# Attention with decay masks: row maxima split on GpSimd, turned onto the stack's partitions, far keys first, max pass 10 slots ahead

## The chip, the cores and the metric

The kernel runs on one core of one Trainium2 chip. The metric is the device time of one execution in microseconds (us), median over runs. Engines are named as in the profile: PE is TensorE (PEld its weight loads), DVE is VectorE, ACT is ScalarE, POOL is GpSimd, SP is SyncE, which issues most DMAs. A letter q behind an engine's name (ACTq, SPq) marks a DMA that this engine issues.

## What is computed

One transformer layer over x of shape (2, 2048, 256): a layer norm, attention with 16 heads of 16 values, an output projection and a residual, then a layer norm, a two-matrix FFN with ternary weights and a residual. The attention weights its scores with a decay that depends on the distance of query and key, one mask per head:

```python
attn_scores = jnp.einsum('bhqd,bhkd->bhqk', q, k) / jnp.sqrt(jnp.float32(D))
time_diffs = jnp.abs(t[:, None] - t[None, :])
decay_masks = dp[:, :, None, None] ** time_diffs[None, None, :, :]
decay_mask = jnp.einsum('hnqk,hn->hqk', decay_masks, mix)
attn_scores = attn_scores * decay_mask[None]
attn_probs = jax.nn.softmax(attn_scores, axis=-1)
out = jnp.einsum('bhqk,bhkd->bhqd', attn_probs, v)
```

The masked scores are wanted twice: once for their maximum over the keys of each query, once, with that maximum subtracted, for the exponential.

## The kernel before, in words

A first block (`token_block`, to about 110 us) makes the layer norm, the projections and the decay tables and builds the first pair of heads. A second block holds attention and the FFN. Attention takes 16 **steps** (2 batches x 8 pairs of heads; `for_steps`, line 810). A step has 4 **units** (2 heads x 2 halves of 1024 queries) of 8 **slots**; in a slot two blocks of 128 keys are worked on, against the 1024 queries of the unit.

Two passes run through the same slots (the tensor block's `step`, lines 1785 to 1817):

- The **scores** (`scores`, line 1649): scores lie transposed, keys on partitions. A key block and a query half that don't share the same half of the sequence ("far") are one matmul of 512 columns per tile, with the decay built into the operands at level 0. A near block is made of levels 1, 2 and 3 (512, 256 and 128 columns) and of its 128 x 128 diagonal square, which is brought in by a transpose (line 1661). The operands are the **stacks** `q_stack` and `k_stack`: 96 rows of high and low f16 parts, and two more rows (96 and 97, `STACK` to `STACK + MAXROWS`) that multiply a constant of the k side with the high and low part of minus the query's maximum over 1024, so that the maximum is subtracted by the matmul itself. A slot has four tiles of 128 x 512 in a ring of three PSUM banks (`tile`); ScalarE takes each through an exponential (line 1379) into `probs`, and a slot later TensorE multiplies `probs` with the values (`values`, line 1687).
- The **max pass** runs `LEAD` = 12 slots ahead (`max_scores`, line 1621): queries on partitions, 128 of them against 2048 keys a slot, in two items of 1024 keys. VectorE multiplies each item with the head's mask and reduces it to a maximum (`max_block`, line 1408; line 1425). The item that holds the diagonal is written to `masked` (two buffers), from which GpSimd copies the diagonal square (`keep_diag`, line 1201; line 1207). TensorE may not run ahead of VectorE by more than the `ring` of two items.

Slots count from 0 to 31 in a step. Eight blocks of the max pass belong to one unit. After the eighth, in slot 4 of every 8 (`RED_SLOT`), VectorE reduces the items to `row_max` (`finish_max`, line 1429; line 1434) and splits it into two f16 parts for all four levels (`split_max`, line 1436; lines 1443 and 1447). In the next slot (`TURN_SLOT`) TensorE transposes the 64 columns of `max_parts` (`turn_max`, line 1641; line 1646) into a tile bank, as one more item of the tile ring between the slot's third and fourth tile; ScalarE copies 64 x 128 values into `max_rows` (`take_turn_max`, line 1346; line 1351) and issues a DMA that lays them out in the two rows of `q_stack` for all four levels (`store_max_rows`, line 1354; line 1357). GpSimd subtracts the maxima from the unit's eight diagonal squares (`diag_minus_max`, line 1209; line 1213). The unit that uses all this starts in the next slot with s % 8 == 0; there TensorE waits for the stacks' loads, that row DMA (`rows_in`) and the diagonals (`diag_ready`), lines 1790 to 1797. Key blocks are taken in their order, 0 to 15, in both halves.

Meanwhile the next pair's operands are built in eight chunks: GpSimd multiplies (line 289), ScalarE casts to f16 (line 302), GpSimd subtracts for the low part (line 308). `pool_slot` and `cast_slot` (lines 1002 to 1007) write out by hand in which slot of a step each of these is issued; each engine works in the order of its program. SyncE's order is written out too (`step`, lines 1099 to 1166): stack 1 at a step's start, the next masks and raw heads when the max pass is done with the old, levels 0 and 1 and then 2 and 3 of stack 0, and last the tables and q and k of the pair after (`builder.load`, line 197). In the last step nothing of this is built and the first pieces of the FFN are mixed into the slots.

Of the kernel before, what the change touches and what calls it, by code (L numbers as in the profile page):

```python
# [792 lines left out]
LEAD = UNIT_SLOTS + 4  # L793
# [4 lines left out]
RED_SLOT, TURN_SLOT = 4, 5  # L798
# [41 lines left out]

def score_parts(block, side):
# [12 lines left out]
def attention_and_ffn_block(nc, a, keep, builder, proj, scr, out):  # L854
# [7 lines left out]
    with ExitStack() as ctx:  # L862
# [17 lines left out]
        max_parts = sb("max_parts", [P, MAXROWS, DEPTH, UNIT_SLOTS], F16)  # L880
        max_rows = sb("max_rows", [MAXROWS * DEPTH * UNIT_SLOTS, P], F16)
        unit = sb("unit", [P, 1])
        zero = sb("zero", [P, 1])
# [56 lines left out]
        max_ready, max_hi, parts_ready = sem("max_ready"), sem("max_hi"), sem("parts_ready")  # L940
# [12 lines left out]
        const_in, zero_ready = sem("const_in"), sem("zero_ready")  # L953
# [4 lines left out]
        LO_ROWS = DEPTH * UNIT_SLOTS  # L958
# [36 lines left out]
        def place(g):  # L995
# [6 lines left out]
        pool_slot = {2: ("product", 0), 4: ("product", 1), 7: ("rest", 0), 8: ("product", 2), 10: ("rest", 1),  # L1002
                     11: ("product", 3), 12: ("rest", 2), 14: ("product", 4), 15: ("rest", 3), 16: ("product", 5),
                     18: ("rest", 4), 19: ("product", 6), 20: ("rest", 5), 22: ("product", 7), 24: ("rest", 6),
                     26: ("rest", 7)}
        cast_slot = {5: (0, 0), 6: (0, 1), 7: (1, 0), 8: (1, 1), 9: (2, 0), 10: (2, 1), 12: (3, 0), 13: (3, 1),
                     15: (4, 0), 16: (4, 1), 17: (5, 0), 18: (5, 1), 20: (6, 0), 21: (6, 1), 23: (7, 0), 24: (7, 1)}

        @block.sync
        def _(sp):  # L1010
# [88 lines left out]
            def step(i, o, more):  # L1099
# [59 lines left out]
                if i + 2 < STEPS:  # L1159
                    builder.load(sp, i + 2)  # L1160
# [33 lines left out]
        def _(pool):  # L1194
# [14 lines left out]
            def diag_minus_max(h, half, count):  # L1209
# [4 lines left out]
                                        ALU.subtract).then_inc(diag_ready, 1)  # L1214

# [53 lines left out]
            for s in range(-LEAD, 0):  # L1269
                keep_diag(s, 0)  # L1270
                if s == TURN_SLOT - UNIT_SLOTS:
                    diag_minus_max(0, 0, 1)
            def step(i, o, more):
                for s in range(SLOTS):
# [3 lines left out]
                    if s % UNIT_SLOTS == TURN_SLOT and (more or u < UNITS):  # L1278
                        diag_minus_max((u // 2) % 2, u % 2, UNITS * i + u + 1)
# [29 lines left out]
        def _(act):  # L1309
# [36 lines left out]
            def take_turn_max(slot, o, count):  # L1346
# [7 lines left out]
            def store_max_rows(h, half, slot, o):  # L1354
# [6 lines left out]
            take_turn_max(TURN_SLOT - UNIT_SLOTS, 0, 1)  # L1361
            store_max_rows(0, 0, TURN_SLOT - UNIT_SLOTS, 0)
            proj.wait_rows(act, GROUPS)
            def step(i, o, more):
# [5 lines left out]
                for s in range(SLOTS):  # L1370
# [3 lines left out]
                    for x in range(4):  # L1374
                        n = tile_item(s, x, o)
                        if turning and x == 3:
                            take_turn_max(s, o, UNITS * i + u + 1)
# [4 lines left out]
                    if turning:  # L1382
                        store_max_rows(u // 2 % 2, u % 2, s, o)
# [23 lines left out]
        def _(dve):  # L1407
# [27 lines left out]

            def split_max(par, count):

                hi, lo = max_parts[:, 0], max_parts[:, 1]
                row = row_max[:, par].unsqueeze(1).broadcast_to([P, DEPTH, UNIT_SLOTS])
                dve.wait_ge(max_ready, count)  # L1440
                if count > 1:
                    dve.wait_ge(rows_in, QUADS * (count - 1))
                nc.vector.scalar_tensor_tensor(out=hi, in0=row, scalar=-1.0 / MAXUNIT,  # L1443
# [445 lines left out]
```

## Time and profile before

| | us |
|---|---|
| runs, median (lowest to highest, 3 runs) | 1913.11 (1912.32 to 1914.3) |
| the profiled execution, its own time | 1910.07 |
| its span, first to last instruction | 1908.3 |
| granted clock of TensorE, mean | 0.95 of full speed |

Durations below are from that one execution. A line such as L1425 is a line of the kernel. "out<-in" names tensors without their buffer numbers; `late` is the shared memory that holds the second stacks and `probs`. In a timeline row the bracket at the end is the idle time just before and what ended it; PE rows with a count merge several matmuls that overlap. PEclk is the granted share of TensorE's clock in a stretch: 1.0 is 2.4 GHz, 0.5 is 1.2 GHz, and a value between is a stretch with both.

### The profile page before, as it was taken

Reading aid. Unit: us, or ns where it says so; the run is one execution under the profiler, and the core shown is the slowest. Engines: PE = TensorE matmul, PEld = TensorE weight load, DVE = VectorE, ACT = ScalarE, POOL = GpSimd, SP = SyncE. Lnnn points to the kernel's source line nnn. Section 1 sums busy time; section 2 is a strip of 40 time slices with the busy share of each in tenths; the row PEclk is TensorE's granted clock in tenths of the full one; section 3 lists DMA queues with packets and bytes.
Section 4 is the critical chain, followed back from the end, with each engine's and each line's share of the span. In section 5 each row is a group of like instructions: output and inputs, shape, how many; then the busy total and the mean of one; then the engine's idle time right before and its main releaser. Section 6 shows DMA issues by size and latency. Waiting matters only on the chain.

```text
span 1908.3 us, 31293 instructions
## 1 busy us (share of the span) xinstructions
PE 1705.1 (89%) x10834; PEld 589.1 (31%) x10834; DVE 1527.7 (80%) x2638; ACT 1427.4 (75%) x2669; POOL 912.7 (48%) x915
## 2 busy tenths in 40 slices
PE   7836899998989899989898989899999999999998
PEld 5401222222222222223232222222222222224666
DVE  5766888787878787878787888888887878796885
ACT  6524878787878787878787878778787878787665
POOL 6733637363636454555545464636373636343010
PEclk9867999999999999999999999999999999999999
DMA  6967574756565665748484757575747575562640
GB/s 206 331 205 187 149 169 126 179 136 170 144 159 146 151 160 146 178 120 198 116 192 131 177 141 173 148 168 144 174 130 183 129 178 143 139 186 59 159 125 34
DMA packets 195217, 300.03 MB, mean 157 GB/s; under 512 B 92114, under 2 KB 115538, under 8 KB 184914
## 3 DMA queue, kind: packets, MB, share of 16 engines
q1 hardware_dynamic: 188980, 296.85, 61.1%
q10 hardware_dynamic: 6080, 1.19, 0.4%
q8 instruction: 86, 1.41, 0.3%
q14 instruction: 71, 0.58, 0.1%
HBM read 152.18 MB, written 42.99 MB: 102 GB/s over the span
## 4 chain that ended last, share of the span: by engine, by line
PE 59%; DVE 15%; issue 9%; DMA 5%; SPq 3%; ACT 2%; POOL 1%; DVEq 0%; ACTq 0%
PE tile L1664 21%; PE ring L1679 20%; PE ring L1633 11%; DVE masked L1425 5%; DMA late<-max_rows 4%; DVE unseen L1425 4%; DVE max_parts L1443 3%; PE tile L1661 2%; PE ring L1749 2%; SPq L233 1%; ACT late L1379 1%; PE tile L1731 1%; SPq L202 1%; DVE qk L1514 1%; DMA raw_scratch<-late 1%
## 5 line engine op out<-in xcount | busy, mean ns | idle before, releaser
L1379 ACT ACTIVATE late<-tile 128x512 f32<-128x512 f32 x2048 | 1107.6, 604 | 321.1 <-PE tile L1664 219.5
L1425 DVE CUSTOM_DVE_ANT_0 masked<-ring,mask 128x1024 f32<-128x1024 f32 x512 | 625.0, 1221 | 180.7 <-PE ring L1633 158.1
L1425 DVE CUSTOM_DVE_ANT_0 unseen<-ring,mask 128x1024 bf16<-128x1024 f32 x512 | 625.0, 1221 | 100.1 <-PE ring L1633 100.1
L1679 PE MATMUL ring<-late,v_ones 128*32 128x512 f32 x4096 | 569.7, 629 | 0.1
L1207 POOL COPY diag<-masked 128x128 f32<-128x128 f32 x512 | 149.0, 291 | 780.3 <-DVE part_max L1425 769.6
L1633 PE MATMUL ring<-k_raw,q_raw 64*128 64x512 f16 x2048 | 351.6, 397 | 88.9 <-DVE part_max L1425 76.7
L1664 PE MATMUL tile<-late 98*128 98x512 f16 (+2 forms) x1280 | 330.0, 345 | 62.2 <-issue 48.0
L1664 PE MATMUL tile<-q_stack,k_stack 98*128 98x512 f16 (+2 forms) x1280 | 316.8, 334 | 11.6 <-ACT late L1379 8.5
L289 POOL TENSOR_TENSOR decayed<-qk,table_in 128x1024 f32<-128x1024 f32 x120 | 284.1, 2367 | 2.4 <-DMA table_in<-table_scratch 2.3
L308 POOL TENSOR_TENSOR lo<-decayed,hi 128x1024 f16<-128x1024 f32 x120 | 256.3, 2136 | 0.0
L1664 PEld LDWEIGHTS tile<-late 98*128 98x128 f16 x1280 | 101.7, 99 | 389.7 <-ACT late L1379 239.7
L1664 PEld LDWEIGHTS tile<-q_stack,k_stack 98*128 98x128 f16 x1280 | 100.0, 98 | 316.0 <-ACT late L1379 214.0
L302 ACT CAST hi<-decayed 128x512 f16<-128x512 f32 (+1 forms) x248 | 158.3, 638 | 21.8 <-DMA late<-lo 10.5
L1633 PEld LDWEIGHTS ring<-k_raw,q_raw 64*128 64x128 f16 x2048 | 91.9, 94 | 267.4 <-DVE part_max L1425 151.0
L1661 PE MATMUL tile<-ident,diag 128*128 128x128 f32 x512 | 143.8, 281 | 0.0
L1679 PEld LDWEIGHTS ring<-late,v_ones 128*32 128x32 f32 x4096 | 82.0, 109 | 170.7 <-issue 130.7
L1213 POOL TENSOR_TENSOR diag<-diag,row_max 128x1024 f32<-128x1024 f32 x64 | 121.4, 1897 | 0.1
L1425 DVE DVE_READ_ACCUMULATOR2_ANT part_max<- 128x1 f32 x1024 | 84.1, 82 | 0.0
L1661 PEld LDWEIGHTS tile<-ident,diag 128*128 128x128 f32 x512 | 72.4, 141 | 6.6
L1218 POOL TENSOR_TENSOR diag<-diag,bo_all 128x1024 f32<-128x1024 f32 x8 | 18.8, 2354 | 110.0 <-DMA diag<-in_x 110.0
L1514 DVE TENSOR_TENSOR qk<-late,diag 128x512 f16<-128x512 f32 x64 | 45.3, 709 | 27.9 <-ACT late L1337 27.9
L1443 DVE SCALAR_TENSOR_TENSOR max_parts<-row_max,zero 128x32 f16<-128x32 f32 x64 | 56.1, 877 | 2.4 <-DVE row_max L1434 0.3
(148 smaller groups left out, 1049.1 us busy)
## 6 DMA issues: line engine op xcount, KB each, us to landing
mask<-mask_row_scratch SPq DMA_DIRECT2D x128, 496.0 KB, 7.5
table_in<-table_scratch SPq DMA_DIRECT2D x64, 256.0 KB, 8.4
q_raw<-raw_scratch SPq DMA_DIRECT2D x128, 128.0 KB
k_stack<-hi SPq DMA_DIRECT2D x64, 256.0 KB, 4.0
q_stack<-hi SPq DMA_DIRECT2D x128, 128.0 KB, 3.8
late<-hi SPq DMA_DIRECT2D x64, 256.0 KB, 8.7
late<-hi SPq DMA_DIRECT2D x128, 128.0 KB, 8.0
out_scratch<-heads_out SPq DMA_DIRECT2D x64, 256.0 KB, 6.2
```

The lines of the kernel that those rows point to most:

```text
L289: ops.tensor_tensor(self.source(c), self.half_view(self.qk[:], level, side), self.factors(level, side), ALU.mult).then_inc(self.decayed_re ...
L302: self.nc.scalar.copy(out, src).then_inc(self.hi_ready, 2 if x is None else 1)
L308: ops.tensor_tensor(self.half_view(self.lo[:, level], level, side), self.source(c), self.half_view(self.hi[:, level], level, side), ALU.su ...
L1207: nc.gpsimd.tensor_copy(diag[h][:, q], masked[:, b % 2, at:at + P]).then_inc(masked_free, 1)
L1213: nc.gpsimd.tensor_tensor(part, part, row_max[:, half].unsqueeze(2).broadcast_to([P, UNIT_SLOTS, P]), ALU.subtract).then_inc(diag_ready, 1)
L1379: nc.scalar.activation(probs[:, (2 * s + x // 2) % 4, x % 2 * 512:(x % 2 + 1) * 512], tile[:, n % TILE_BANKS], ACT.Exp, scale=1.0 / (SCALE ...
L1425: nc.vector.tensor_tensor_reduce(out=masked[:, b % 2] if diagonal else unseen[:], in0=pair, in1=factor, scale=1.0, scalar=-3.0e38, op0=ALU ...
L1443: nc.vector.scalar_tensor_tensor(out=hi, in0=row, scalar=-1.0 / MAXUNIT, in1=zero[:].unsqueeze(2).broadcast_to([P, DEPTH, UNIT_SLOTS]), op ...
L1633: last = nc.tensor.matmul(ring[:, 2 * (n % RING) + r], q_raw[h][rows, q * P:(q + 1) * P], k_raw[h][rows, k], start=True, stop=True)
L1661: last = nc.tensor.matmul(out, diag[h][:, kb], ident[:], is_transpose=True, start=(j == 0), stop=True, skip_group_check=True)
L1664: last = nc.tensor.matmul(out, k_stack[h][:, level, kb * P:(kb + 1) * P], q_stack[h][:, half, level, first - half * HALF:first - half * HA ...
L1679: last = nc.tensor.matmul(acc[row:row + ROWS], v_ones[h][:, t % BLOCKS], probs[:, t % 4, qt * 512:(qt + 1) * 512], start=(j % UNIT_SLOTS = ...
```

## The change

The maxima are split by GpSimd instead of VectorE, three small operations into an f16 tile that holds only the two parts of 8 x 128 maxima. TensorE turns them with eight transposes, block by block, whose output lies on PSUM partitions 96 and 97, the partitions of the stack's two rows, 1024 f16 values wide. ScalarE copies that straight into level 0 of `q_stack`, and the DMA that follows only copies level 0 to levels 1 to 3. Keys are taken far half first (`key_block`), so that a unit's first four slots need level 0 alone; the waits for levels 2 and 3 of the stacks, for that DMA and for the diagonals go to the unit's fifth slot (`NEAR_SLOT`). The max pass leads by 10 slots, which puts reduction, turning and the diagonals' subtraction into slots 5, 6 and 7 of every 8. The slots of products, rests and casts are written anew, and SyncE issues the loads of the pair after next before the last output store and the second half of stack 0. `last_turn` gives the tile item of a turn, for the waits on ScalarE's copy.

```diff
-LEAD = UNIT_SLOTS + 4
+LEAD = UNIT_SLOTS + 2
...
-RED_SLOT, TURN_SLOT = 4, 5
+RED_SLOT = (UNIT_SLOTS - 1 - LEAD) % UNIT_SLOTS
+TURN_SLOT = RED_SLOT + 1
+NEAR_SLOT = UNIT_SLOTS // 2
+DIAG_SLOT = UNIT_SLOTS - 1
...
+def key_block(t, half):
+
+    return (t + (1 - half) * UNIT_SLOTS) % BLOCKS
...
+        pool_slot = {3: ("product", 0), 6: ("product", 1), 8: ("rest", 0), 9: ("product", 2), 11: ("rest", 1),
+                     12: ("product", 3), 14: ("rest", 2), 16: ("product", 4), 17: ("rest", 3), 18: ("product", 5),
+                     19: ("rest", 4), 20: ("product", 6), 22: ("rest", 5), 24: ("product", 7), 25: ("rest", 6),
+                     27: ("rest", 7)}
+        cast_slot = {5: (0, 0), 7: (0, 1), 9: (1, 0), 10: (1, 1), 11: (2, 0), 12: (2, 1), 13: (3, 0), 15: (3, 1),
+                     17: (4, 0), 18: (4, 1), 19: (5, 0), 20: (5, 1), 21: (6, 0), 23: (6, 1), 25: (7, 0), 26: (7, 1)}
...
                     load_max_pass(1, i + 1)
+                if i + 2 < STEPS:
+                    sp.wait_ge(builder.decayed_ready, CHUNKS * (i + 2))
+                    builder.load(sp, i + 2)
                 store_out(i, 2)
...
                     load_q(0, 1, 1)
-                if i + 2 < STEPS:
-                    builder.load(sp, i + 2)
...
+            def split_max(par, slot, o, count):
+
+                hi, lo = max_parts[:, :, 0], max_parts[:, :, 1]
+                pool.wait_ge(max_ready, count)
+                if count == 1:
+                    pool.wait_ge(unit_ready, 1)
+                if count > 1:
+                    pool.wait_ge(exp_done, last_turn(slot + 1, o) + TILE_BANKS + 1)
+                nc.gpsimd.tensor_tensor(max_neg[:], row_max[:, par], down_unit[:].broadcast_to([P, UNIT_SLOTS]), ALU.mult
+                                        ).then_inc(neg_ready, 1)
+                pool.wait_ge(neg_ready, count)
+                nc.gpsimd.tensor_copy(hi, max_neg[:]).then_inc(max_hi, 1)
+                pool.wait_ge(max_hi, count)
+                nc.gpsimd.tensor_tensor(lo, max_neg[:], hi, ALU.subtract).then_inc(parts_ready, 1)
...
-                    if s % UNIT_SLOTS == TURN_SLOT and (more or u < UNITS):
+                    if s % UNIT_SLOTS == RED_SLOT and (more or u < UNITS):
+                        split_max(u % 2, s, o, UNITS * i + u + 1)
+                    if s % UNIT_SLOTS == DIAG_SLOT and (more or u < UNITS):
                         diag_minus_max((u // 2) % 2, u % 2, UNITS * i + u + 1)
...
-                act.wait_ge(rows_in, QUADS * (count - 1))
-                nc.scalar.copy(max_rows[:], tile[0:MAXROWS * LO_ROWS, n % TILE_BANKS, 0:P // 2].bitcast(F16)
-                               ).then_inc(exp_done, 1)
...
+                nc.scalar.copy(q_stack[h][STACK:STACK + MAXROWS, half, 0],
+                               tile[STACK:STACK + MAXROWS, n % TILE_BANKS].bitcast(F16)).then_inc(exp_done, 1)
...
-                act.dma_start(q_stack[h][STACK:STACK + MAXROWS, half], max_rows[:]).then_inc(rows_in, QUADS)
+                act.dma_start(q_stack[h][STACK:STACK + MAXROWS, half, 1:DEPTH],
+                              q_stack[h][STACK:STACK + MAXROWS, half, 0].unsqueeze(1).broadcast_to([MAXROWS, DEPTH - 1, HALF])
+                              ).then_inc(rows_in, QUADS)
...
-                        split_max(u % 2, UNITS * i + u + 1)
...
-                nc.tensor.transpose(tile[0:MAXROWS * LO_ROWS, n % TILE_BANKS, 0:P // 2].bitcast(F16),
-                                    max_parts[:].rearrange("p r l b -> p (r l b)"), keep["ident16"][:]).then_inc(tile_full, 1)
+                for b in range(UNIT_SLOTS):
+                    last = nc.tensor.transpose(tile[STACK:STACK + MAXROWS, n % TILE_BANKS, b * P // 2:(b + 1) * P // 2].bitcast(F16),
+                                               max_parts[:, b], keep["ident16"][:])
+                last.then_inc(tile_full, 1)
...
-                u, kb = t // BLOCKS, t % BLOCKS
+                u = t // BLOCKS
                 h, half = u // 2, u % 2
+                kb = key_block(t % BLOCKS, half)
...
-                        for done in (*(k_in[u // 2] if u % 2 == 0 else ()), *q_in[u // 2][u % 2]):
+                        pe.wait_ge(exp_done, last_turn(TURN_SLOT + s, o) + TILE_BANKS + 1)
+                        for done in (k_in[u // 2][0], q_in[u // 2][u % 2][0]):
                             pe.wait_ge(done, PART_DMAS * QUADS * (i + 1))
...
+                    if s % UNIT_SLOTS == NEAR_SLOT:
+                        u = s // UNIT_SLOTS
+                        for done in (k_in[u // 2][1], q_in[u // 2][u % 2][1]):
+                            pe.wait_ge(done, PART_DMAS * QUADS * (i + 1))
                         pe.wait_ge(rows_in, QUADS * (UNITS * i + u + 1))
                         pe.wait_ge(diag_ready, UNITS * i + u + 2)
```

## Rows read from the trace of the kernel before

**Rows 1.** The page's first part: engine, busy us (share of the span), instructions.

```profile
PE 1705.1 (89%) x10834; PEld 589.1 (31%) x10834; DVE 1527.7 (80%) x2638; ACT 1427.4 (75%) x2669; POOL 912.7 (48%) x915
```

**Rows 2.** The page's fourth part: the chain of waits, by engine and by line.

```profile
PE 59%; DVE 15%; issue 9%; DMA 5%; SPq 3%; ACT 2%; POOL 1%; DVEq 0%; ACTq 0%
...
PE tile L1664 21%; PE ring L1679 20%; PE ring L1633 11%; DVE masked L1425 5%; DMA late<-max_rows 4%; DVE unseen L1425 4%; DVE max_parts L1443 3%; PE tile L1661 2%; PE ring L1749 2%; SPq L233 1%; ACT late L1379 1%; PE tile L1731 1%; SPq L202 1%; DVE qk L1514 1%; DMA raw_scratch<-late 1%
```

**Rows 3.** Windows, line 1379 (exponentials) alone, steps 1 to 14: start:end, us, busy (count).

```profile
265.72:1660.72 1395.00, 969.70 (x1792) 0.96 0.63 155
```

**Rows 4.** Windows, step 8: start:end, length, busy (count) PE, PEld, DVE, ACT, POOL; PEclk, DMA share, GB/s.

```profile
967.02:980.71 13.69, 13.68 (x96) 4.50 (x94) 12.06 (x22) 11.26 (x22) 5.45 (x7) 1.00 1.04 224
...
980.71:984.81 4.10, 3.02 (x19) 0.76 (x17) 4.07 (x7) 3.01 (x6) 2.60 (x3) 1.00 1.00 222
...
990.18:1003.75 13.57, 13.57 (x88) 3.88 (x87) 12.23 (x23) 12.73 (x27) 9.39 (x10) 1.00 0.61 179
...
1003.75:1008.32 4.57, 3.12 (x22) 1.09 (x21) 4.57 (x6) 3.02 (x8) 2.17 (x3) 1.00 0.24 93
...
1011.06:1015.02 3.96, 2.87 (x24) 1.04 (x22) 3.57 (x7) 2.68 (x6) 3.47 (x3) 1.00 0.08 25
...
1015.02:1028.70 13.68, 13.67 (x96) 4.45 (x94) 10.90 (x20) 12.90 (x25) 9.25 (x10) 1.00 0.71 149
...
1028.70:1033.42 4.72, 3.07 (x19) 0.76 (x17) 4.68 (x7) 3.05 (x7) 3.22 (x3) 1.00 0.15 53
...
1033.42:1037.57 4.15, 4.15 (x18) 0.65 (x16) 2.02 (x5) 2.18 (x5) 2.81 (x3) 0.59 0.92 257
...
1037.57:1042.85 5.28, 2.70 (x18) 0.67 (x16) 4.15 (x8) 2.68 (x6) 2.15 (x3) 1.00 0.69 197
...
1042.85:1046.62 3.77, 3.77 (x17) 0.67 (x16) 0.91 (x1) 3.14 (x7) 0.52 (x1) 0.62 0.13 52
...
1057.81:1060.68 2.87, 2.87 (x22) 1.10 (x21) 2.62 (x5) 2.43 (x5) 0.80 (x2) 1.00 0.86 223
```

**Rows 5.** The tile max_parts: ns minimum/median/maximum, first and last start, form.

```profile
L1443 DVE SCALAR_TENSOR_TENSOR max_parts<-row_max,zero x64: 191/192/2004, 141.7 to 1715.4; 128x32 f16<-128x32 f32 x64
...
L1447 DVE SCALAR_TENSOR_TENSOR max_parts<-row_max,max_parts x64: 191/192/2040, 141.9 to 1715.6; 128x32 f16<-128x32 f32 x64
```

**Rows 6.** Timeline, step 8, slot 12 to 13: start, us, engine, line, operation.

```profile
1002.98 2.14 POOL L308 TENSOR_TENSOR lo<-decayed,hi 128x1024 f16<-128x1024 f32 x1
...
1003.13 2.04 DVE L1447 SCALAR_TENSOR_TENSOR max_parts<-row_max,max_parts 128x32 f16<-128x32 f32 x1
```

**Rows 7.** Timeline, step 8, slots 21 to 24, the row DMA and TensorE's next score.

```profile
1030.98 0.56 ACTq L1357 DMA_DIRECT2D late<-max_rows  x1
...
1042.37 0.81 PE L1664 MATMUL tile<-late 98*128 98x512 f16 x3 [2.58 <-issue]
```

**Rows 8.** Timeline, step 8, slots 28 and 29: reduction and transpose.

```profile
1056.91 0.17 DVE L1434 TENSOR_REDUCE row_max<-part_max 128x8 f32<-128x16 f32 x1
...
1059.13 0.11 PEld L1646 LDWEIGHTS tile<-ident,max_parts 128*64 128x64 f16 x1 [0.84 <-ACT late L1379]
```

**Rows 9.** Groups by line and form: busy us, mean ns | idle before, releaser.

```profile
L289 POOL TENSOR_TENSOR decayed<-qk,table_in 128x1024 f32<-128x1024 f32 x120 | 284.1, 2367 | 2.4 <-DMA table_in<-table_scratch 2.3
...
L1326 ACT CAST mask<-ring 128x1024 f16<-128x1024 f32 x8 | 8.1, 1011 | 3.4 <-PE ring L1715 3.4
...
L1351 ACT COPY max_rows<-tile 64x128 f16<-64x128 f16 x64 | 16.5, 258 | 32.5 <-PE tile L1646 31.9
...
L480 POOL TENSOR_TENSOR power<-power 32x8 f32<-32x8 f32 x1 | 0.2, 195 | 0.1
```

**Rows 10.** Timeline, last step: four matmuls of 128 columns.

```profile
1742.43 0.39 PE L1773 MATMUL ring<-ident,hi 128*128 128x128 f16 x4
```

**Rows 11.** Timeline, step 0: the first score, and the cast of slot 5.

```profile
152.75 0.48 PE L1664 MATMUL tile<-q_stack,k_stack 98*128 98x256 f16 x2 [3.08 <-DMA q_stack<-max_rows]
...
180.93 0.62 ACT L302 CAST hi<-decayed 128x512 f16<-128x512 f32 x1 [10.54 <-DMA late<-lo]
```

More of the change, by code:

```diff
@@ L838, in items_done, with last_turn @@
     return RING_STEP * o + ring_item(slot, ITEMS - 1) + AHEAD_ITEMS + 1
+def key_block(t, half):
+    return (t + (1 - half) * UNIT_SLOTS) % BLOCKS
+def last_turn(slot, o):
+    if slot < 0 or (slot == TURN_SLOT and o == 0):
+        return 0
+    return turn_item(slot - UNIT_SLOTS, o) if slot >= UNIT_SLOTS else turn_item(slot + SLOTS - UNIT_SLOTS, o - 1)
 def score_parts(block, side):
@@ L879, in attention_and_ffn_block @@
         row_max = sb("row_max", [P, 2, UNIT_SLOTS])
-        max_parts = sb("max_parts", [P, MAXROWS, DEPTH, UNIT_SLOTS], F16)
-        max_rows = sb("max_rows", [MAXROWS * DEPTH * UNIT_SLOTS, P], F16)
+        max_neg = sb("max_neg", [P, UNIT_SLOTS])
+        max_parts = sb("max_parts", [P, UNIT_SLOTS, MAXROWS], F16)
         unit = sb("unit", [P, 1])
-        zero = sb("zero", [P, 1])
+        down_unit = sb("down_unit", [P, 1])
         warm = sb("warm", [P, 1])
@@ L1270, in _ @@
                 keep_diag(s, 0)
-                if s == TURN_SLOT - UNIT_SLOTS:
+                if s == RED_SLOT - UNIT_SLOTS:
+                    split_max(0, s, 0, 1)
+                if s == DIAG_SLOT - UNIT_SLOTS:
                     diag_minus_max(0, 0, 1)
@@ L1434, in finish_max @@
                 nc.vector.tensor_reduce(row_max[:, par], part_max[:, par], AX.X, ALU.max).then_inc(max_ready, 1)
[L1436 to L1443, printed above, removed]
-                                               in1=zero[:].unsqueeze(2).broadcast_to([P, DEPTH, UNIT_SLOTS]),
-                                               op0=ALU.mult, op1=ALU.add).then_inc(max_hi, 1)
-                dve.wait_ge(max_hi, count)
-                nc.vector.scalar_tensor_tensor(out=lo, in0=row, scalar=-1.0 / MAXUNIT, in1=hi, op0=ALU.mult,
-                                               op1=ALU.subtract).then_inc(parts_ready, 1)
             def invert(g):
@@ L1559, in _ @@
                 max_block(s, 0)
-                if s % UNIT_SLOTS == RED_SLOT and s + LEAD >= UNIT_SLOTS:
+                if s == RED_SLOT - UNIT_SLOTS:
                     finish_max(0, items_done(s, 0), None)
-                    split_max(0, 1)
             def step(i, o, more):
@@ L1678, in products @@
                         row = (2 * par + qt) * ROWS
-                        last = nc.tensor.matmul(acc[row:row + ROWS], v_ones[h][:, t % BLOCKS],
+                        last = nc.tensor.matmul(acc[row:row + ROWS], v_ones[h][:, key_block(t % BLOCKS, u % 2)],
                                                 probs[:, t % 4, qt * 512:(qt + 1) * 512],
@@ L1780, in _ @@
                 max_scores(s, range(ITEMS), 0)
-                if s % UNIT_SLOTS == TURN_SLOT and s + LEAD >= UNIT_SLOTS:
+                if s == TURN_SLOT - UNIT_SLOTS:
                     turn_max(s, 0, 1)
```

28 lines of the change are left out of this document (11 added, 17 removed).

## The prediction

> **What bounds the kernel now.** I read the engine shares first: TensorE is busy 89% of the span [rows 1]. The chain of waits is on TensorE for 59%, but also 15% on VectorE, 9% in "issue" and 5% on DMA, where it names the DMA that carries the row maxima into the stack (4%) and the line on VectorE that splits them (3%) [rows 2]. So I went to the attention stage, 14 whole steps of which take 1395.00 us: 1792 exponentials, four to a slot, 448 slots, 99.64 us a step [rows 3].
>
> Then one step in stretches, cut at the first exponential of a slot [rows 4]. Three stretches of five slots have TensorE busy without a gap (13.68 of 13.69 us) at full clock: 40.94 us for 15 slots, **2.73 us a slot, 87.4 a step**. VectorE has 10.9 to 12.2 and ScalarE 11.3 to 12.9 busy us in the same stretches, so TensorE is the limit there. Of the missing 12.3 us, 11.6 sit in eight slots. Over 2.73 each:
> - slots 5, 13, 21 (4.10, 4.57, 4.72): +1.37, +1.84, +1.99. These are the slots in which a unit's maxima are reduced, split and turned; TensorE is busy only 3.0 to 3.1 us in them.
> - slot 15 (3.96): +1.23, and slot 23 (5.28): +2.55, each the last before a unit starts.
> - slots 22 and 24 (4.15, 3.77): +1.42 and +1.04 with TensorE busy throughout, at a granted clock of 0.59 and 0.62: part of each at the lower level (1.2 GHz), right after the stalls of 21 and 23.
> - slot 29 (2.87), also a turning slot: +0.14 only.
>
> Why does slot 29 cost a tenth of the other three? The two split operations on VectorE take 0.19 us at the least and median, but up to 2.00 and 2.04 [rows 5]. In slot 13 the second one runs from 1003.13 for 2.04 us and ends at 1005.17, 0.05 us after a GpSimd subtraction that began at 1002.98 and took 2.14 [rows 6]. VectorE is held by GpSimd's operation, and the max pass, and TensorE behind it, with it. In slot 29 GpSimd has no product or rest to do. The slots ahead of a unit's start wait for the row DMA: issued at 1030.98, TensorE goes on at 1042.37 after an idle 2.58, 11.4 us later; slots 22 and 23 hide only part of it [rows 7].
>
> **The change, part by part.**
> - *Split moved to GpSimd.* Removed from VectorE: two operations a unit, 0.38 us free, up to 2.2 held. The VectorE operations that stay are not held: in two clean stretches 22 and 23 of them take 12.06 and 12.23 us, beside 5.45 and 9.39 us of GpSimd [rows 4]. Added on GpSimd: three operations of 8 columns, 0.195 us each by the nearest row (32x8) [rows 9], 0.6 us, and some 0.3 for the waits between them. In the clean turning slot the reduction starts at 1056.91 (0.17 long) and TensorE loads the transpose at 1059.13 [rows 8]: 2.22 us, so 2.22 - 0.17 - 0.9 = 1.15 are to spare and TensorE does not wait. Behind GpSimd's new wait stand the next diagonal copy (VectorE needs it only two blocks later) and the products; GpSimd has no product or rest in slots 5, 13, 21 and 29 by the new table.
> - *Turning.* One transpose becomes eight of 128 columns. Four such matmuls in a row take 0.39 us [rows 10], one alone 0.219 [rows 9], so they start 0.055 apart: seven more, +0.39 on TensorE. ScalarE's copy grows from 128 columns (0.258) to 1024 on two partitions; a 1024-column copy from PSUM takes 1.011 [rows 9]: +0.75. Nothing (ScalarE is busy 11.26 of 13.69 us in five slots without casts [rows 4], so 0.49 idle a slot, and the new cast table has none in turning slots) and all of it are the bounds. There are three tile banks: after the transposes TensorE has one score tile (0.22 by the spacing above), the next slot's four max matmuls (0.44 to 0.88, as their two row halves run side by side or not) and another tile before it needs the bank that this copy holds, 0.9 to 1.3 us against a copy that ends some 1.2 after; the copy then puts off the exponential behind it and so the next bank. That is nearer the middle than either end; I take +0.40. A turning slot is then 2.87 + 0.39 + 0.40 = 3.66, **0.93 over a plain slot** (bounds 3.26 and 4.01).
> - *Maxima into level 0 by ScalarE, spread to levels 1 to 3 by DMA; far keys first.* A unit's first four slots read level 0 alone. Its start waits for a copy made a slot and a half earlier: nothing. The DMA is now awaited in the unit's fifth slot, some five slots (13.6 us) after its issue instead of two; where it is slowest it takes the 11.4. So +1.23 and +2.55 go. What is late next: the diagonal (GpSimd subtracts in slot 7, TensorE wants it in slot 12) and levels 2 and 3 of the stacks, wanted four slots later than now.
> - *Clock.* With the stalls of 21 and 23 gone, +1.42 and +1.04 go too. After the stalls of 5 and 13, of 1.4 and 1.8 us, the rows that follow show 1.00 [rows 4], so stalls of about half a microsecond should not lower it.
> - *SyncE.* Six loads of the next pair go ahead of the output store and nine stack loads, behind a wait for the last product (slot 24). The stack loads wait for the rests (slot 27) anyway, and the store is needed two units later: nothing. The moved casts and products are the same in number: nothing.
> - *Lead 10 for 12.* Two slots fewer of max pass at the start; but step 0 stands in slot 5 until 180.93 for a load into the second stack [rows 11], which depends on no score. I count nothing; the bound is a gain of 8: two slots at VectorE's 12.06 / 5 = 2.41 [rows 4] and the 3.08 that the first score waits for the row DMA [rows 11]. At the end two more slots carry four 512-column max matmuls, at most 2 x 4 x 0.22 = 1.8; I take 1.
>
> **The sum.** A step: 87.4 + 4 x 0.93 = 91.1, against 99.64: 8.5 saved, x14 = 120. Step 0 after its load: 26 slots took 265.7 - 181.5 = 84.2; 26 x 2.73 + 3 x 0.93 = 73.8: 10.4 saved. The last step has no products to hold VectorE: three turning slots 0.79 dearer each, and the 1 us: 3.4 lost. Together 127. The profiled execution took 1910.07 (span 1908.3), so 1783; the median of the runs is 3.04 higher: **1786**. With the cheap turning slot: 89.5 a step, 1762, and with all of the start 1754. With the dear one: 92.5 a step, 1808.
>
> **Rivals.**
> - *The clock still falls.* If the new stalls of turning slots keep a drop of the kind of slots 22 and 24, 2.46 us a step come back: x14 = 34, **1820**. For it: TensorE still waits there. Against: slots 5 and 13.
> - *The spread lands late.* It decides from about 14 us on. From slot 29 on and in the next step's first slots the DMA engines are 0.86 to 1.04 busy [rows 4]. At 20 us one unit a step waits 6: +84, **1870**. Against: its 11.4 us came under a like load. The Trainium skill (DMA: Bandwidth & Descriptors, Rules for kernel authors) says that a small outermost dimension confines a DMA to as many engines; by it the two rows ride on two engines behind everything queued there, as today's would not less, so the 11.4 agrees but bounds nothing.
> - *VectorE stays held.* If it is not the split alone that GpSimd's work holds up, the 1.37 to 1.99 stay: 4.8 us a step, +67, **1853**. Against: the two clean stretches of the part on the split.
> - *Slower: the split comes late.* GpSimd runs in order. If it is two large operations behind when the maxima come (2.4 + 2.1 us), the split ends 4.5 - 1.15 = 3.4 us after TensorE wants it, in three units, and each such stall costs 1.4 us more of low clock: 3 x 4.8 = 14.4 us a step, x14 = 202, **1988**. One operation behind costs about 1.2 and still gains; the sign turns where each of three units loses 3 us (127 / 14 / 3). For it: products and rests stand in slots 16 to 20 without a break, 2.37 us for a product [rows 9] and a diagonal copy beside it. Against: 2.73 a slot holds that. The Trainium skill (GPSIMD Engine Reference, Performance versus the Vector engine) keeps elementwise work on VectorE, GpSimd being about 1.96 times slower: an estimate by it makes the split 2 x 1.96 x 0.19 = 0.75 us; the rows here give 0.6 for three operations, and both fit the 1.15 to spare, so it is the queue and not the operation that this case hangs on.
>
> **How the numbers follow.** The forecast gets 0.74, the clock 0.08, a late spread 0.05, VectorE held 0.06, slower 0.05, no difference 0.02. A measurement of this kernel can tell 0.2% (3.8 us). The first four are faster: 0.93. The range goes from 1756 (the cheap turning slot and most of the start) past the dear one and the clock's case to 1838; beyond it lie the late spread, the held VectorE, the slower and the null case, 0.18.
>
> **What would show it.** Right: slots 5, 13, 21 gone from the stalls and slots 6, 14, 22, 30 all alike at 3.3 to 4.0; no wait of TensorE on the row DMA; clock 1.00 through slots 21 to 25; about 91 us a step; VectorE's line for the split gone and no other of its lines slower. Wrong: TensorE waiting for GpSimd's split or, in a unit's fifth slot, for a DMA; ScalarE's wide copy over 1.1 us; a step above 96.

## The result, and the profile after

The changed kernel takes **1934.06 us** (median of 4 runs, 1927.67 to 1937.88); the kernel before, run beside it, 1913.7 (4 runs, 1912.32 to 1920.8). The ratio is **1.0095, interval 1.0055 to 1.0136**: slower by about 1%. Forecast were 1786, range 1756 to 1838, and 0.05 for slower. The profiled execution took 1927.67 us (span 1925.9), 17.6 more than that of before.

First the page's engine shares and its chain by engine, which answer to [rows 1, 2]:

```profile
PE 1697.7 (88%) x11282; PEld 614.7 (32%) x11282; DVE 1448.3 (75%) x2510; ACT 1468.2 (76%) x2669; POOL 952.1 (49%) x1107
...
PE 41%; SPq 20%; DMA 19%; DVE 5%; ACT 4%; issue 3%; POOL 2%; ACTq 0%; DVEq 0%; POOLq 0%
```

VectorE has gone from 15% of the chain to 5%, as it should; but DMA and SyncE's queue have come from 8% to 39%. The same 14 steps as in [rows 3], then step 8 cut by slots (columns as in [rows 4]; 0 to 2, 3, 4, 5, 6, 7 to 13, 14, 15 to 21, 22, 23 to 29, 30, 31):

```profile
255.37:1672.94 1417.57, 972.98 (x1792) 0.95 0.64 153
...
966.44:974.38 7.94, 7.94 (x50) 1.97 (x48) 7.20 (x13) 6.91 (x13) 1.81 (x4) 1.00 1.03 211
974.38:985.90 11.52, 2.98 (x19) 0.99 (x18) 4.14 (x8) 2.17 (x4) 2.87 (x3) 0.79 0.79 189
985.90:990.88 4.98, 4.98 (x21) 1.36 (x20) 1.10 (x1) 2.17 (x4) 0.00 (x0) 0.50 0.55 134
990.88:993.90 3.02, 3.02 (x22) 1.03 (x20) 1.96 (x6) 2.56 (x5) 0.86 (x4) 0.95 0.88 154
993.90:997.50 3.60, 3.43 (x31) 1.47 (x28) 2.82 (x5) 3.20 (x6) 2.61 (x2) 1.00 0.33 91
997.50:1016.43 18.93, 18.93 (x125) 5.62 (x124) 16.40 (x30) 18.16 (x35) 13.23 (x15) 1.00 0.51 150
1016.43:1020.00 3.57, 3.40 (x31) 1.45 (x28) 2.87 (x5) 3.20 (x6) 1.79 (x3) 1.00 0.13 52
1020.00:1038.75 18.75, 18.75 (x125) 5.64 (x125) 16.29 (x30) 18.01 (x35) 16.29 (x17) 1.00 0.42 97
1038.75:1042.36 3.61, 3.44 (x31) 1.48 (x28) 2.83 (x5) 3.20 (x6) 2.44 (x3) 1.00 0.56 90
1042.36:1061.21 18.85, 18.85 (x124) 5.60 (x124) 16.32 (x30) 16.97 (x32) 10.84 (x14) 1.00 0.80 189
1061.21:1064.86 3.65, 3.48 (x32) 1.48 (x30) 2.95 (x5) 3.18 (x5) 0.48 (x2) 1.00 1.02 214
1064.86:1067.50 2.64, 2.64 (x19) 0.76 (x19) 1.89 (x5) 2.17 (x4) 1.24 (x2) 1.00 1.01 261
```

A step is 101.26 us (1417.57 / 14), not 91.1. Everywhere but in slots 3 to 5 the forecast stands: plain slots 2.64 to 2.70 by the mean of each row, turning slots 3.57 to 3.65 and all alike, no wait at a unit's start, clock 1.00. All of the loss lies in unit 0: slot 3 takes 11.52 and slot 4, at clock 0.50, 4.98 (12.21 and 4.58 by the mean of the 14 steps). (A slot is cut at ScalarE's first exponential, so a wait of TensorE in its slot 4 shows in slot 3.) The view of waits, and TensorE's timeline in step 9, say for what:

```profile
PE tile L1687 <- DMA q_stack<-lo: 128.9, 14, 12.1
...
POOL decayed L289 <- DMA table_in<-table_scratch: 71.1, 15, 7.5
...
1086.31 0.48 PE L1687 MATMUL tile<-q_stack,k_stack 98*128 98x256 f16 x2 [8.66 <-DMA q_stack<-lo]
```

In 14 steps TensorE waits 9.2 us on average for levels 2 and 3 of stack 0. Against before: the start and step 0 gain 10.2 us (first exponential of step 1 at 255.4 instead of 265.6), 14 steps lose 22.5 (1417.57 - 1395.09, cut alike), and the last step with what follows it loses the other 5.3.

**Why so late?** SyncE issues these loads at 1057.0 to 1066.8, slots 28 to 31; the last that unit 0 needs goes out at 1060.74, 17 us before TensorE wants it (at 1077.65, the end of its wait less 8.66). The issues of that stretch in the DMA view (count, KB each, median us to landing):

```profile
k_stack<-hi SPq DMA_DIRECT2D x2, 256.0 KB, 19.5
q_stack<-hi SPq DMA_DIRECT2D x4, 128.0 KB, 11.7
out_scratch<-heads_out SPq DMA_DIRECT2D x1, 256.0 KB, 26.2
k_stack<-lo SPq DMA_DIRECT2D x1, 256.0 KB, 13.0
q_stack<-lo SPq DMA_DIRECT2D x2, 128.0 KB, 23.8
```

Loads of one size, issued within 10 us, take 12 us or 24 (the six of 128 KB). The trace counts the arrivals on a semaphore in order of time, so a share that lags shows only at the last load of each semaphore; q_stack<-lo is the third of three. Some of the 16 engines are about 12 us behind the rest. Which, is in the step's own row of slot 14: SyncE has issued nothing for 9 us, and the DMA share is still 0.13, 52 GB/s. 0.13 x 16 = **two engines**, 26 GB/s each. Slots 6 to 8 issued one head's raw q and k: 4 loads of 128 KB and 4 of 64, 786 kB, 15.1 us at 52 GB/s. In the changed kernel the other head's raw loads are issued from 1038.0, its masks from 1044.9, and then, without a pause, the six loads and the nine. The two engines carry their sixteenth of all these behind 15 us of raw loads.

### The profile page after: what moved, and what is told of

It reads as the page before. It is cut to its first block, busy times and chain, and to the rows that moved or that the text cites. A ratio compares the mean times of both kernels' runs of the same rounds, so it can differ in the third digit from the quotient of the medians.

```text
span 1925.9 us, 32286 instructions
## 1 busy us (share of the span) xinstructions
PE 1697.7 (88%) x11282; PEld 614.7 (32%) x11282; DVE 1448.3 (75%) x2510; ACT 1468.2 (76%) x2669; POOL 952.1 (49%) x1107
## 4 chain that ended last, share of the span: by engine, by line
PE 41%; SPq 20%; DMA 19%; DVE 5%; ACT 4%; issue 3%; POOL 2%; ACTq 0%; DVEq 0%; POOLq 0%
DMA q_stack<-lo 18%; PE ring L1702 14%; PE tile L1687 14%; PE ring L1653 7%; SPq L233 5%; SPq L86 4%; SPq L213 3%; SPq L77 3%; SPq L202 2%; SPq L75 2%; PE ring L1772 2%; POOL decayed L289 2%; DVE masked L1462 2%; PE tile L1684 1%; PE tile L1754 1%
## 5 line engine op out<-in xcount | busy, mean ns | idle before, releaser
L1702 PE MATMUL ring<-late,v_ones 128*32 128x512 f32 x4096 | 559.6, 618 | 5.2 <-issue 5.1
L1687 PE MATMUL tile<-q_stack,k_stack 98*128 98x512 f16 (+2 forms) x1280 | 331.5, 345 | 134.1 <-DMA q_stack<-lo 128.9
L1653 PE MATMUL ring<-k_raw,q_raw 64*128 64x512 f16 x2048 | 335.2, 393 | 31.2 <-DVE part_max L1462 18.8
L1687 PE MATMUL tile<-late 98*128 98x512 f16 (+2 forms) x1280 | 315.0, 331 | 8.2 <-ACT late L1416 8.1
L1653 PEld LDWEIGHTS ring<-k_raw,q_raw 64*128 64x128 f16 x2048 | 86.7, 93 | 196.3 <-issue 101.6
L1684 PE MATMUL tile<-ident,diag 128*128 128x128 f32 x512 | 147.8, 289 | 0.0
L1370 ACT ACTIVATE diag<-tile,b_col 128x512 f16<-128x512 f32 x48 | 33.1, 689 | 33.3 <-PE tile L1754 33.3
```

The lines of the kernel that those rows point to most:

```text
L1653: last = nc.tensor.matmul(ring[:, 2 * (n % RING) + r], q_raw[h][rows, q * P:(q + 1) * P], k_raw[h][rows, k], start=True, stop=True)
L1684: last = nc.tensor.matmul(out, diag[h][:, kb], ident[:], is_transpose=True, start=(j == 0), stop=True, skip_group_check=True)
L1687: last = nc.tensor.matmul(out, k_stack[h][:, level, kb * P:(kb + 1) * P], q_stack[h][:, half, level, first - half * HALF:first - half * HA ...
L1702: last = nc.tensor.matmul(acc[row:row + ROWS], v_ones[h][:, key_block(t % BLOCKS, u % 2)], probs[:, t % 4, qt * 512:(qt + 1) * 512], start ...
```

## The experiments

Times of the kernel before beside them: 1919.2 (E1 to E4), 1914.8 (E5, E6, E7, E9) and 1919.4 us (the rest).

**E1: only the order undone.**

```diff
-                if i + 2 < STEPS:
-                    sp.wait_ge(builder.decayed_ready, CHUNKS * (i + 2))
-                    builder.load(sp, i + 2)
                 store_out(i, 2)
...
                     load_q(0, 1, 1)
+                if i + 2 < STEPS:
+                    builder.load(sp, i + 2)
```

> Three theories of the stall of about 9.4 us in unit 0's fourth slot. A, two-engine backlog: the raw loads of the max pass move by two of the 16 DMA engines and need some 20 us; the six loads of the pair after next now follow them at once, so these two engines carry a backlog through every later load, and the last sixteenth of the stack's levels 2 and 3 lands 12 to 16 us after the rest. B, volume: 2 MB of loads stand ahead of the stack loads, whichever engines carry them. C, lead: the max pass is two slots nearer, so the raw loads and the rests come two and one slots later, and the order plays no part. Here the six loads go back behind the stack loads. A and B both expect the stall gone: 14 steps of about 91 us, 1780 to 1800 us in all. C expects the stall to stay: 1900 us or more.

1928.36 us, ratio 1.0048 (1.0028 to 1.0068). A and B missed by 130 us, and C has the number. But the stall has changed place, victim and cause: slot 3 is a plain 2.68, slot 5 takes 13.01. The waits of E1, then GpSimd, ScalarE and TensorE in step 9:

```profile
POOL decayed L289 <- DMA table_in<-table_scratch: 142.6, 15, 13.7
...
ACT hi L302 <- DMA late<-lo: 139.9, 14, 13.5
...
1087.67 2.34 POOL L289 TENSOR_TENSOR decayed<-qk,table_in 128x1024 f32<-128x1024 f32 x1 [9.53 <-DMA table_in<-table_scratch]
...
1093.70 0.62 ACT L302 CAST hi<-decayed 128x512 f16<-128x512 f32 x1 [9.89 <-DMA late<-lo]
...
1094.86 1.01 PE L1666 MATMUL tile<-ident,max_parts 128*2 128x128 f16 x8 [9.34 <-ACT late L1415]
```

Now the tables and, behind them, the loads of stack 1 (`late`) stand last, and their lagging share lands last. GpSimd and ScalarE both wait for it in slot 5. GpSimd's first product waits for a table until 1087.67 and holds up the diagonal copies and the split, which is done by 1091.2. ScalarE's first cast overwrites what the loads of stack 1 read, and waits for them until 1093.70. This second wait ends last: the exponentials stand behind the cast, and TensorE goes on at 1094.86. The order only chooses who is late. No theory had said that; the time alone would have spoken for the wrong one.

**E2: raw loads over 16 engines, order as changed.** The rows of both operands are permuted alike, so the products are the same.

```diff
-            sp.dma_start(q_raw[to], bass.AP(raw.tensor, q_at + x * part, [[0, 2], [SEQ, HEAD_DIM], [1, SEQ]])
+            sp.dma_start(q_raw[to], bass.AP(raw.tensor, q_at + x * part, [[SEQ, HEAD_DIM], [0, 2], [1, SEQ]])
...
-                         bass.AP(raw.tensor, k_at + r * HALF, [[part, 2], [SEQ, HEAD_DIM], [1, HALF]])
+                         bass.AP(raw.tensor, k_at + r * HALF, [[SEQ, HEAD_DIM], [part, 2], [1, HALF]])
```

> The order stays as in the changed kernel, but each raw load is laid out so that its outer loop has 16 rows instead of 2 (rows permuted alike in both operands of the max pass, so the products are the same). A (two-engine backlog) expects the raw loads to drain in about 3 us, every landing within 2 us of its neighbours, the stack's levels 2 and 3 landed by slot 2, no stall: 1780 to 1810 us. B (volume) and C (lead) expect 1900 us or more, the stall as it was. If the outer loop does not set how many engines carry a load, the raw loads still show 3 landings instead of 16 and nothing changes.

**1747.72 us, ratio 0.9096 (0.9069 to 0.9123).** The 14 steps; slots 3, 4 and 14 of step 8; raw loads of q, then levels 2 and 3, in the DMA view of two stretches:

```profile
234.78:1491.46 1256.68, 972.48 (x1792) 1.00 0.67 171
...
871.05:873.73 2.68, 2.68 (x20) 0.84 (x19) 2.40 (x5) 2.17 (x4) 0.85 (x2) 1.00 1.05 245
873.73:876.47 2.74, 2.74 (x22) 1.05 (x21) 2.38 (x5) 2.17 (x4) 2.06 (x2) 1.00 0.92 245
...
901.76:905.33 3.57, 3.40 (x31) 1.45 (x28) 2.87 (x5) 3.19 (x6) 1.78 (x3) 1.00 0.00 0
...
q_raw<-raw_scratch SPq DMA_DIRECT2D x4, 128.0 KB, 2.7
...
k_stack<-hi SPq DMA_DIRECT2D x2, 256.0 KB, 10.0
q_stack<-hi SPq DMA_DIRECT2D x4, 128.0 KB, 9.6
k_stack<-lo SPq DMA_DIRECT2D x1, 256.0 KB, 9.9
q_stack<-lo SPq DMA_DIRECT2D x2, 128.0 KB, 9.9
```

Slots 3 and 4 are plain, the clock is 1.00, slot 14 has no transfer left, a raw load lands after 2.7 us, and hi and lo land alike. A step is 89.76 us. A holds; B and C, which left the raw loads out, fall.

**E3 and E9: the order alone, on the kernel before; E9 with 16-row raw loads as well.**

```diff
+                if i + 2 < STEPS:
+                    sp.wait_ge(builder.decayed_ready, CHUNKS * (i + 2))
+                    builder.load(sp, i + 2)
                 store_out(i, 2)
...
-                if i + 2 < STEPS:
-                    builder.load(sp, i + 2)
```

> The kernel before with this one part of the change: the six loads of the pair after next, behind a wait for the last product, ahead of the output store and the nine stack loads; raw loads, lead and splits as before. All levels are wanted at unit 0's start there. A (two-engine backlog): the raw loads start two slots earlier than in the changed kernel, so the lagging engines come to the end of the stack loads about when unit 0 starts, give or take 3 us: 1895 to 1950 us. B (volume, whichever engines): the stack loads land 8 to 10 us later than in the kernel before, behind unit 0's start by 5 us or more in each of 14 steps: 1975 us or more. C (lead): no loss, 1905 to 1920 us.

> The kernel before with the six loads ahead of the stack loads (2102 us with the raw loads as they were) and 16-row raw loads. A (two-engine backlog): the 8.7 and 4.5 us waits in slots 31 and 0 go with the lag, and it comes within 15 us of the kernel before with 16-row raw loads alone. B (volume): the stack loads still land 8 to 10 us later and are all wanted at the unit's start: 60 us or more above that kernel.

E3 took 2102.28 us, 1.0957 (1.0898 to 1.1015): B's number, and 150 us above A's. E9 took 1791.3, 2 us from E6 below, where B wanted 60 more: all of E3's loss goes with the lag. A's size was wrong twice over. Unit 0's start alone costs 7.5 us a step where A had 3 at the most: slots 31 and 0 take 8.69 and 4.37 us on average, against 2.83 and 2.72 in the kernel before. And other starts stall as well: slots 7 and 8 take 6.5 and 4.6 (2.7 and 3.2 before), slots 23 and 24 7.0 and 4.6 (6.1 and 4.2 before). For what these wait I did not take apart.

**E4: lead 12 in the changed kernel** (`LEAD = UNIT_SLOTS + 4`).

> The changed kernel with a lead of 12 slots instead of 10; all else, the order on SyncE too, stays. A (two-engine backlog): the raw loads start about 5.4 us earlier, so the stall shrinks by about that, from 9.4 to some 4 us: 1830 to 1870 us. B (volume): the six loads wait for the last product and not for the max pass, so the stall stays: 1915 to 1940 us. C (lead): the stall goes entirely, 1775 to 1800 us.

1927.51 us, 1.0048 (1.0026 to 1.0071): no effect. That is B's number, which E2 and E9 rule out; C falls, and A's size is wrong too. The raw loads did not come earlier. They were issued at 1044.38, in slot 21 as with lead 10 (1038.03), because SyncE is held ahead of them by the loads of levels 0 and 1, which wait for GpSimd's rests, not for the max pass. The waits of SyncE in E4:

```profile
SPq L1151 <- POOL lo L308: 311.0, 15, 22.0
```

**E5: 16-row raw loads and the order undone** (E1 and E2 together).

> The changed kernel with 16-row raw loads and the six loads put back behind the stack loads. If the order costs nothing once no engine lags (A): 1740 to 1755 us, as with 16-row raw loads alone. If the order has a price of its own (B), 15 us or more below that; if the table loads are wanted sooner than the back position gives them (the product waited for the table when the order alone was undone), above 1765 us.

1754.83 us: A. It is 7.1 us above E2, as slot 5 takes 3.45 on average instead of 2.77, 0.5 us a step in all: without a lag the new order gains a little.

**E6: 16-row raw loads in the kernel before** (E2's diff alone).

> The kernel before with the raw loads' outer loop of 16 rows and nothing else. If the two-engine backlog is also what made the row transfers of the maxima land 11 us late there (they are carried by two engines as well), the waits of slots 15 and 23 (3.8 us a step) and the fallen clock behind them (2.5 us) go, while VectorE's hold (5.2 us) stays: about 93.4 us a step, 1815 to 1840 us. If the row transfers are slow of themselves (512 pieces of 256 bytes), nothing much changes: 1895 to 1920 us. The distance from this time to that of the changed kernel with the same edit (1747.7 us) is what the change itself is worth without the backlog; the prediction's sum gives the hold, the rest of the waits and the turning, some 3 to 6 us a step or 40 to 85 us.

1793.38 us, ratio 0.9358 (0.9326 to 0.9389), more than expected. Step 8, slots 13, 15, 21, 22, 23 and 24:

```profile
930.90:935.48 4.58, 3.12 (x22) 1.09 (x21) 4.58 (x6) 3.05 (x7) 2.18 (x3) 1.00 0.02 4
938.22:941.05 2.83, 2.83 (x24) 1.05 (x23) 2.44 (x5) 2.56 (x5) 2.35 (x3) 1.00 0.00 0
954.72:959.44 4.72, 3.07 (x19) 0.76 (x17) 4.68 (x7) 3.06 (x7) 3.22 (x3) 1.00 0.51 142
959.44:962.04 2.60, 2.60 (x18) 0.58 (x16) 1.90 (x5) 2.17 (x4) 2.46 (x3) 1.00 0.94 243
962.04:964.80 2.76, 2.76 (x18) 0.66 (x16) 2.53 (x5) 2.62 (x5) 0.66 (x2) 1.00 1.00 393
964.80:967.97 3.17, 3.17 (x22) 0.81 (x24) 2.78 (x5) 3.06 (x7) 2.39 (x2) 1.00 0.25 100
```

Against [rows 4]: the holds of slots 13 and 21 stay within 0.01 us, the waits of 15 and 23 and the fallen clock of 22 and 24 are gone. So the row DMA of before was not slow of itself in these slots: it stood behind the raw loads. (At 16 KB it is 64 pieces of 256 bytes, not 512.) A step falls from 99.6 to 92.9 us. The rest comes from step 0 (94.9 us instead of 112) and the start, which I had not counted. The change itself, freed of the lag, is worth 1793.4 - 1747.7 = **45.7 us**.

**E7: 16-row raw loads, the split back on VectorE** (the three operations of `split_max` with `nc.vector` in place of `nc.gpsimd`, behind `finish_max`).

> The changed kernel with 16-row raw loads, the split of the maxima back on VectorE in the same three operations. Hold theory: a VectorE operation with two operands in SBUF is held while GpSimd's long operations run; by this kernel's table GpSimd's product runs over into slot 21 by some 1.6 us and into slot 13 by some 0.7 us, and slots 5 and 29 are free, so TensorE waits in one or two units of four, up to 1.5 us each: 1755 to 1790 us, the split's operations 1 us or longer there. Rival, no hold: the three operations take about 0.1 us each everywhere and the time stays within 5 us of 1747.7 us.

1747.15 us: the rival, no hold, with 0.17 us an operation. The tile max_parts in E7 (ns minimum/median/maximum):

```profile
L1465 DVE CAST max_parts<-max_neg x64: 173/174/175, 132.9 to 1553.9; 128x8 f16<-128x8 f32 x64
L1467 DVE TENSOR_TENSOR max_parts<-max_neg,max_parts x64: 170/171/1778, 133.1 to 1554.1; 128x8 f16<-128x8 f32 x64
```

The one length near 1.8 us is the hold, in the last step:

```profile
1553.92 1.90 POOL L1228 TENSOR_TENSOR diag<-diag,row_max 128x1024 f32<-128x1024 f32 x1
...
1554.06 1.78 DVE L1467 TENSOR_TENSOR max_parts<-max_neg,max_parts 128x8 f16<-128x8 f32 x1
```

Of the 128 operations above, only this one and the cast just before it have an operation of GpSimd beside them. In the new table GpSimd has no product or rest in slots 5, 13, 21 and 29, so in the other steps nothing meets them. The operations are also narrower than in [rows 5], 8 columns for 32, but the one that met a long operation was held all the same.

**E8: 16-row raw loads, the late waits at a unit's first slot again** (`if s % UNIT_SLOTS == 0:` for `NEAR_SLOT`).

> The changed kernel with 16-row raw loads, and the waits for levels 2 and 3, the spread rows and the diagonal at a unit's first slot again (key order kept). If these come later than the unit's start, as in its trace (levels 2 and 3 of stack 0 land some 4 us into slot 0, GpSimd's diagonal operation ends up to 1 us into a unit's first slot), each step pays 4 to 5 us in unit 0 and 0 to 2 us in each of the others: 1800 to 1860 us. Rival, TensorE's lead over ScalarE covers it: within 10 us of 1747.7 us.

1870.14 us, 122 above E2, 77 above E6 and 10 above the range. Its waits:

```profile
PE tile L1687 <- DMA q_stack<-q_stack: 49.7, 14, 5.8
PE tile L1687 <- POOL diag L1228: 42.6, 47, 1.6
```

Each step waits up to 5.8 us for unit 0's spread rows, which I had left out of the sum, and in other units for the diagonal. Far keys first, with the waits moved to the fifth slot, is what lets the rest of the change pay.

**E10: 16-row raw loads, lead 12.**

> The changed kernel with 16-row raw loads and a lead of 12 slots instead of 10, GpSimd's table left as it is. The prediction counted the lead as nothing in a whole step, a gain of up to 8 us at the start and 1 us lost at the end. With 12 and the backlog there was no difference (1927.5 against 1934.1 and 1928.4 us). Expected the same here: 1735 to 1760 us; the split is then queued behind GpSimd's rests in three units of four, which may cost TensorE up to 1.4 us each but is made up in the slots after. If the lead itself holds something up, above 1765 us.

1747.12 us. On balance the lead is worth nothing: with 12 the first exponential comes 4.4 us later than in E2 (142.3 against 137.9) and a step takes 90.04 us instead of 89.76, but step 0 and the end are 9 us shorter. With 12 the changed kernel loses to the same lag (E4).

**E11 and E12: half the dose.** The changed kernel with only k, or only q, laid over 16 engines; rows stay where they were. E11 (E12 does the same for q):

```diff
-RAW_DMAS = 8
+RAW_DMAS = 12
...
-            sp.dma_start(k_raw[to].rearrange("p u x -> p (u x)"),
-                         bass.AP(raw.tensor, k_at + r * HALF, [[part, 2], [SEQ, HEAD_DIM], [1, HALF]])
-                         ).then_inc(done, QUADS)
+            for u in range(2):
+                half = slice(to.start + u * HEAD_DIM, to.start + (u + 1) * HEAD_DIM)
+                sp.dma_start(k_raw[half].rearrange("p u x -> p (u x)"),
+                             bass.AP(raw.tensor, k_at + u * part + r * HALF, [[SEQ, HEAD_DIM], [1, HALF]])
+                             ).then_inc(done, QUADS)
```

> The changed kernel with only the raw loads of k laid over 16 engines (two loads of 16 rows each instead of one of 2 x 16, rows where they were; four more issues on SyncE a head), those of q left on two. The k pieces are 64 of 2048 bytes at 0.08 us for each of the two engines, 5.1 us of the 15.4 us that a head's raw loads take them alone. If the stall is the backlog of these two engines, it shrinks with it, by about 5 us of 9.4, and the fallen clock with it in part: 1835 to 1865 us. If something else of the 16-row layout took the stall away (the order of the rows, or the loads being finished sooner for the max pass), it goes at once or not at all: under 1770 or over 1910 us.

> The same for q alone: 64 of 4096 bytes at 0.16 us for each of the two engines, 10.2 of the 15.4 us, go. By the backlog theory the lag falls below the stall's length: no stall or one under 2 us, 1745 to 1790 us. If the lag does not go with the bytes on the two engines, 1900 us or more.

E11 took 1848.95 us (0.9652, 0.9605 to 0.9698), E12 1754.84 (0.916, 0.9122 to 0.9198): both inside. In E11:

```profile
PE tile L1689 <- DMA q_stack<-lo: 55.4, 14, 5.9
```

The stall falls from 9.2 to 4.0 us a step, by 5.2 where the k bytes at two engines' rate gave 5.1; E12 has none. The stall follows the bytes on the two engines, not the place of the rows or the order.

## Why the prediction was wrong

**The step that failed** is SyncE's: "The stack loads wait for the rests (slot 27) anyway, and the store is needed two units later: nothing." The issue times were right (slots 28 to 31, after rest 7). The landing was taken from them: I costed the move by what SyncE waits for and by what stands ahead in its queue, not by what the DMA engines still had to carry. In the kernel before SyncE stopped after the masks until the rests were done, and the two engines emptied in that pause; the change fills it. The next sentence failed with it: "The moved casts and products are the same in number: nothing." The same in number, but rest 3 moved from slot 15 to 17; the loads of levels 0 and 1 wait for it, and the second head's raw loads stand behind these, so they moved from slot 19 to 21 (E4: with lead 12 too). SyncE's issues in step 8, from the masks on, in the kernel before, the changed kernel and E1:

```profile
1031.34 6.29 SPq L86 DMA_DIRECT2D mask<-mask_row_scratch  x4
...
1052.84 0.59 SPq L233 DMA_DIRECT2D k_stack<-hi  x1
...
1044.93 5.83 SPq L86 DMA_DIRECT2D mask<-mask_row_scratch  x4
1050.80 1.34 SPq L202 DMA_DIRECT2D qk<-q_scratch  x1
...
1045.61 5.84 SPq L86 DMA_DIRECT2D mask<-mask_row_scratch  x4
...
1056.77 0.59 SPq L233 DMA_DIRECT2D k_stack<-hi  x1
```

From the end of the masks to the next load pass, with one store between, 15.2 us in the kernel before, 5.3 in E1, where the old order stands with the new slots, and none in the changed kernel. Either move takes away most of the pause: the order alone costs 183 us in E3, and undoing it alone gains nothing in E1. No run puts the slots of the rests back alone, so how the loss divides between the two is not shown. "What is late next: ... levels 2 and 3 of the stacks" named the victim, and "in a unit's fifth slot, for a DMA" the sign, both without a price.

The evidence lay in [rows 4]. Slot 24 shows a DMA share of 0.13 and 52 GB/s, slot 15 0.08: two engines still at work long after the last issue. I read these rows for their clock only. The Trainium skill (DMA: Bandwidth & Descriptors, Rules for kernel authors) says that a DMA whose outermost dimension has c entries is confined to at most c engines, and gives a leading broadcast of c copies as its example. The prediction weighed that rule for the two spread rows and asked for no other load of that form; the raw loads of q begin with just such a broadcast, `[0, 2]`. The trace agrees: 0.13 of 16 engines with 2 outermost, 2.7 us to landing with 16. The Trainium skill (DMA: Bandwidth & Descriptors, Why a DMA increments its semaphore by 16 and not by 1) adds that SyncE's kind of DMA takes the lowest-numbered engines; by that all loads confined to two would share the same two. No trace here names engines; that the row DMA's delay went with the raw loads (E6) fits it.

Point by point, with the lag out of the way (E2):
- *The sum's mechanism holds, its size was a little short.* Forecast 91.1 us a step, measured 89.76; turning slots forecast 3.66 (3.26 to 4.01), measured 3.57 to 3.65; plain slots 2.69 on average, not 2.73.
- *Turning.* ScalarE's wide copy takes 1.005 us by the median, forecast 1.011. The two additions to slot 29's 2.87 were less well placed than their sum: TensorE is busy 3.40 to 3.48 us of a turning slot, 0.53 to 0.61 more for a forecast 0.39, and idle 0.17 for a forecast 0.40. The 0.219 us of a single matmul of 128 columns stands in none of [rows 9], but in this row of the kernel before:

```profile
L1664 PE MATMUL tile<-late 98*128 98x128 f16 x256 | 56.0, 219 | 0.0
```

- *Split on GpSimd.* 0.20 us an operation as forecast, and TensorE waits for it once, 0.5 us in all. But the move was not needed (E7): the gain that I gave to it belongs to the slot table.
- *Row DMA.* The waits went, by moving (E8) and by freeing its engines (E6). Its 11.4 us were read as its own latency; they were the queue.
- *Clock.* 1.00 through slots 21 to 25, as forecast; in the changed kernel the 9 us stall takes it down to between 0.50 and 0.71 in slot 4 instead. At 4.58 against 2.72 us by the mean of the 14 steps that costs 1.9 a step. The forecast's reason was weaker than it looked: [rows 4] does not show slots 6 and 14, which follow the stalls of 5 and 13, and step 8 is one of the good ones. In the kernel before slot 14 stands at 1.00 in nine of the 14 steps and at 0.60 to 0.67 in five, as here in step 3:

```profile
507.67:511.93 4.26, 4.26 (x23) 1.06 (x21) 2.11 (x5) 2.17 (x5) 3.94 (x3) 0.60 0.13 50
```

  And of slot 24's +1.04 only some 0.6 was clock: at 1.00 it takes 3.17 (E6).
- *Start and end.* In the changed kernel step 0 and the start gain 10.2 (forecast 10.4), and that the numbers meet is luck: 9.4 come from the start, which was counted at nothing, and 0.9 from step 0, which was to give all and stands 15 us in slot 5. In E2 the first exponential is at 137.9 instead of 153.6; about 6 of that go with the raw loads (153.6 to 147.9 in E6, 144.2 to 137.9 in E2) and 4.4 with the lead (E10); the rest was not taken apart.
- *The rival "slower"* was another mechanism (a late split) and did not occur. None of the rivals held a late stack load, so 0.93 for faster was too much.

## What to carry to other kernels

When a load is moved ahead in a queue, ask what every DMA engine still has to carry at that moment, not only what the queue waits for: a pause of the issuing engine may be the time in which a few laden engines empty. Here a DMA share of 0.13, two sixteenths, in a stretch without issues was two engines working off a backlog, and loads of one size that landed either promptly or some 12 us late were its sign at the other end. Look at such loads' outermost dimension before anything is re-timed: here two swapped dimensions gave 6.4% on the kernel before, and turned a 1% loss of this change into 9.0% gained.

## What was not expected of the hardware

- Two engines carry 52 GB/s together; a lag of theirs of about 12 us is passed on to the 16-engine loads queued behind, and only the last load of each semaphore shows it.
- After a stall of 9 us the whole next slot ran at a granted clock of 0.50 in six of 14 steps and at 0.57 to 0.71 in the others. After a slot with a stall of 1.4 us (slot 5 of the kernel before) the next slot kept 1.00 in all steps; after one of 1.8 us (slot 13) the same kernel gave 1.00 in nine steps and 0.60 to 0.67 in five, and in E6, where slot 13 is as long, 0.60 in two.
- The same operation on VectorE with two operands in SBUF took 0.17 us by the median and 1.78 at the most, when an operation of GpSimd had begun 0.14 us before it (E7).
